# Four-layer conditional residual kernel in float32: GpSimd's splits of x in quarters, and its sums of layer-0 weights in halves

## What is computed

```python
# layer 0: one 256x256 weight matrix per row, mixed from 8
w = einsum('bg,got->bot', cond_8, weight * mask)
x = x + einsum('bnt,bot->bno', x, w) + bias
# layer 1: one of 8 experts per row (argmax), H = 512
x = x + (silu(x @ wu.T + bu) * (x @ wg.T + bg)) @ wd.T + bd
# layer 2: two of 8 experts per row (softmax weights) and a shared one, I = 1024
x = x + sum_u we[u] * ((gelu_tanh(x @ gate[u]) * (x @ up[u])) @ down[u])
# layer 3: base matrix plus LoRA mixed from 8 experts of rank 16
x = x + x @ (W_base + 2 * mixed_lora).T + b_base
```

## Time and profile before

| | us |
|---|---|
| median of 3 runs | 536.03 |
| lowest and highest | 536.0, 538.26 |
| span of the profiled execution, first to last instruction | 535.1 |
| median less that span | 0.9 |
| busy: PE, DVE, ACT, POOL | 506.0, 362.2, 241.3, 98.3 |

### The profile page before, as it was taken

The page is one execution under the profiler, slowest core; times in us unless marked ns, Lnnn a source line. Parts: engine busy times, 40 slices in busy tenths (PEclk is TensorE's granted clock), DMA queues, the critical chain, the costliest instruction groups (busy, mean ns, idle before and its releaser), DMA issues.

```text
span 535.1 us, 7145 instructions
## 1 busy us (share of the span) xinstructions
PE 506.0 (95%) x2155; PEld 405.9 (76%) x2155; DVE 362.2 (68%) x559; ACT 241.3 (45%) x372; POOL 98.3 (18%) x63
## 2 busy tenths in 40 slices
PE   6797988898999999899999998999999989999997
PEld 2475865686888888688888886888888778888886
DVE  4999999969865575755656557565665665656545
ACT  3464552462444445344444543444454444454430
POOL 1968694209400000200000002000000200000000
PEclk9999998998999999989999998999999999999999
DMA  8931312131423323232332332223223233230004
GB/s 253 385 96 32 106 49 72 53 106 59 119 88 103 103 88 91 69 105 88 99 107 80 98 108 67 88 88 118 88 88 110 66 105 101 88 92 25 0 1 158
DMA packets 20604, 51.38 MB, mean 96 GB/s; under 512 B 2928, under 2 KB 3568, under 8 KB 20592
## 3 DMA queue, kind: packets, MB, share of 16 engines
q1 hardware_dynamic: 20592, 51.24, 30.6%
HBM read 49.13 MB, written 2.10 MB: 96 GB/s over the span
## 4 chain that ended last, share of the span: by engine, by line
PE 85%; DVE 8%; issue 4%; DMA 2%; SPq 1%; ACT 1%; DVEq 0%
PE act_ps L290 10%; PE lin_ps L290 9%; PE lin_ps L291 9%; PE acc_ps L290 9%; PE lin_ps L292 9%; PE acc_ps L291 9%; PE act_ps L292 9%; PE act_ps L291 9%; PE acc_ps L292 9%; DMA w<-w_in 2%; DVE w_lo L619 1%; DVE hid_lo L637 1%; DVE w_sum L583 1%; DVE w_lo L611 1%; DVE hid L631 1%
## 5 line engine op out<-in xcount | busy, mean ns | idle before, releaser
L619 DVE TENSOR_TENSOR w_lo<-raw,w_hi 128x384 fp32r<-128x384 f32 (+1 forms) x222 | 152.5, 692 | 0.0
L629 DVE TENSOR_TENSOR hid<-lin_ps,act 128x512 f32<-128x512 f32 x96 | 66.2, 690 | 123.5 <-PE lin_ps L292 123.5
L429 ACT ACTIVATE hid_hi<-hid 128x512 fp32r<-128x512 f32 x112 | 70.8, 632 | 128.8 <-DVE hid L629 96.9
L423 ACT ACTIVATE act<-act_ps 128x512 f32<-128x512 f32 x96 | 57.4, 598 | 120.5 <-PE act_ps L292 120.5
L290 PE MATMUL act_ps<-x_hi,w_hi 128*128 (+1 forms) x228 | 90.0, 395 | 18.4 <-issue 13.5
L637 DVE TENSOR_TENSOR hid_lo<-hid,hid_hi 128x512 fp32r<-128x512 f32 x112 | 83.4, 745 | 21.8 <-ACT hid_hi L429 21.7
L417 ACT ACTIVATE w_hi<-raw 128x768 fp32r<-128x768 f32 x112 | 93.9, 838 | 0.0
L290 PE MATMUL lin_ps<-x_hi,w_hi 128*128 (+1 forms) x228 | 90.7, 398 | 0.0
L291 PE MATMUL lin_ps<-x_lo,w_hi 128*128 (+1 forms) x228 | 90.5, 397 | 0.0
L292 PE MATMUL lin_ps<-x_hi,w_lo 128*128 (+1 forms) x228 | 90.4, 397 | 0.0
L292 PE MATMUL act_ps<-x_hi,w_lo 128*128 (+1 forms) x228 | 89.5, 393 | 0.0
(11 more groups left out here) (91 smaller groups left out, 399.0 us busy)
## 6 DMA issues: line engine op xcount, KB each, us to landing
raw<-w_in SPq DMA_DIRECT2D x112, 384.0 KB, 3.0
w<-w_in SPq DMA_DIRECT2D x8, 256.0 KB, 7.6
x<-x_in SPq DMA_DIRECT2D x4, 512.0 KB, 8.2
out<-x SPq DMA_DIRECT2D x7, 256.0 KB, 2.4
mask<-mask_in SPq DMA_DIRECT2D x1, 256.0 KB, 6.6
base<-base_in SPq DMA_DIRECT2D x1, 256.0 KB, 10.1
out<-x SPq DMA_DIRECT2D x2, 128.0 KB, 2.2
lora_b<-lora_b_in SPq DMA_DIRECT2D x1, 128.0 KB, 6.9
```

The costliest lines, as they stand in the source:

```text
L423: act_e.activation(act[:, j % 2, :], act_ps[:, j % 2, :], func, bias=bias).then_inc(act_ready, 1)
L429: act_e.activation(hid_hi[:, j % 2, :], hid[:, j % 2, :], ACT.Copy).then_inc(hid_hi_ready, 1)
L619: ins = dve.tensor_tensor(w_lo[:, j % SPLIT, a:z], raw[:, j, a:z], w_hi[:, j % SPLIT, a:z].bitcast(F32), ALU.subtract)
L629: ins = dve.tensor_tensor(hid[:, j % 2, :], lin_ps[:, j % 2, :], act[:, j % 2, :], ALU.mult)
```

## The change

`split_lo` and `split_both` run over four quarters of 256 columns (`quarter`) in place of one instruction of 1024. The semaphores rise by 1 after every second quarter, and split_lo waits block by block. In `sum_w0` the addition of 512 columns becomes two of 256, and the semaphore rises after the second. The multiplication L793, the masking L782 and the weights of layer 3 stay as they are. No instruction changes its engine or its place in the order.

```diff
+            QT = T // 2
+            def quarter(t, b, q):
+                return t[:, b * CB * T + q * QT:b * CB * T + (q + 1) * QT]
             def split_lo(b, layer):
                 hi, lo, row = (x_hi, x_lo, b) if layer else (x0_hi, x0_lo, b % 2)
-                pool.wait_ge(x_hi_ready[layer], (b + 1) * CB)
-                pool.tensor_tensor(x_row(lo, row), x_row(x_flat, b), x_row(hi, row).bitcast(F32),
-                                   ALU.subtract).then_inc(x_lo_ready[layer], CB)
+                for q in range(CB * 2):
+                    if q % 2 == 0:
+                        pool.wait_ge(x_hi_ready[layer], b * CB + q // 2 + 1)
+                    ins = pool.tensor_tensor(quarter(lo, row, q), quarter(x_flat, b, q),
+                                             quarter(hi, row, q).bitcast(F32), ALU.subtract)
+                    if q % 2 == 1:
+                        ins.then_inc(x_lo_ready[layer], 1)
             def split_both(b, layer):
-                pool.tensor_copy(x_row(x_hi, b), x_row(x_flat, b)).then_inc(x_hi_ready[layer], CB)
+                for q in range(CB * 2):
+                    ins = pool.tensor_copy(quarter(x_hi, b, q), quarter(x_flat, b, q))
+                    if q % 2 == 1:
+                        ins.then_inc(x_hi_ready[layer], 1)
                 split_lo(b, layer)
...
-                        pool.tensor_tensor(w0_sum[:, b, :], w0_sum[:, b, :], w0_term[:, :],
-                                           ALU.add).then_inc(w0_pool, 1)
+                        for c in range(CB):
+                            cut = slice(c * D, (c + 1) * D)
+                            ins = pool.tensor_tensor(w0_sum[:, b, cut], w0_sum[:, b, cut], w0_term[:, cut], ALU.add)
+                        ins.then_inc(w0_pool, 1)
```

## The result

The changed kernel takes 513.79 us (median of 4 runs, 512.99 to 515.93) against 536.58 (4 runs, 536.0 to 538.26). The ratio is 0.9576, with a 95% interval of 0.9548 to 0.9603: 4.2% faster. The forecast was 515.5, within 509.5 to 522.0.

A forecast was written before the change was run, and what follows sets the result against it. TensorE (PE) bounds the kernel, busy 506.0 of 535.1 us, losing time to VectorE held by long GpSimd instructions and to low clock. Gains 14.1 + 6.4 = 20.5 give a 514.6 span, 515.5 median; range 509.5 to 522.

The forecast's parts named there:

- Turns at the boundary: VectorE instructions with two SBUF inputs wait for GpSimd's current instruction, then get in at every instruction boundary, needing 0.41 us.
- the mask rows: Trace at 77 us: between GpSimd instructions without pause, VectorE's w_lo ended at 77.45 and the mask took 1.03, not 0.74.
- the rival of the train: GpSimd's quarters run without letting VectorE in; row-end waits grow by 1.1 us in five episodes: 541.5 us, chance 0.05.
- Layer 2: Row-end episodes at 122, 224, 326 (4.0 us each) and 427 us (2.1) go: gain 14.1 us.
- The spare time: Row end at 224 us: w_lo complete at 223.1, TensorE wants it at 223.66, 0.6 us to spare.
- The two parts of the price: Each layer-2 row loses 4.0 us: 2.08 of TensorE waiting and 1.9 of low clock after it.
- The one at 103 us: TensorE's wait at 103 us, the same episode as at 224, goes with 0.3 to 0.5 to spare: gain 2.3 us.
- Layer 1: With layer 0, from 26.03 to 113.35 us: 13.9 us lost, 8.4 possible to win, 6.4 booked after a debit.
- The waits at 52 and 77: TensorE's layer-1 waits for w_lo go: 1.0 us at 52, 1.9 at 77, plus 1.9 for low clock behind 77.
- the debit of 2.0: Layer 1: 2.0 us taken off for row 3's mask, 2.5 late, and VectorE meeting GpSimd's layer-2 quarters past 90 us.
- The 0.9 between median and span: The median was taken to stand 0.9 us above the profiled span, turning 514.6 into the forecast 515.5.
- The halves of the sums: Halved layer-0 additions shorten VectorE's w_lo waits in layer 1; their gain was counted within the 8.4 us possible there.

The follow-up runs named there:

- casts_quartered: The kernel before with only the casts of x in quarters, each x_lo subtraction and the sums whole: 523.39 us, ratio 0.9738.
- subs_quartered: The kernel before with only the x_lo subtractions in quarters, each cast and the sums whole: 517.60 us, ratio 0.9639.
- sum_halves: The kernel before with only the additions of the layer-0 sums in halves, x in instructions of 1024: 534.82 us, ratio 0.9962.
- halves: The kernel before with x in two instructions of 512 columns, the sums whole: 519.88 us, ratio 0.9691.
- x_quarters: The changed kernel without the halved additions, so only x in quarters: 513.03 us, ratio 0.9548 to the kernel before.
- the finest cut: The kernel before with x in eight instructions of 128 columns, the sums whole: 516.14 us, ratio 0.9625.
- one wait more: x_quarters with GpSimd's layer-2 splits of rows 0 and 1 held until row 2 of layer 1 is added: 511.00 us, 0.9523 of the kernel before.

## Why the prediction was right

**Turns at the boundary: right.** The whole forecast hung on the mask rows, and casts_quartered and subs_quartered confirm it, each with a number of its own (1.42 and 2.41 us for the two w_lo). The Trainium skill's sentence (GPSIMD Engine Reference, section Instruction dispatch), that consecutive Pool instructions are no barrier between its cores, gave the rival of the train; no run here shows a train. Whether the cores wait for each other at a boundary can't be seen in these traces; in the rows shown, a waiting VectorE instruction got in at each.

**Layer 2: right, 14.1 forecast and 14.4 measured.** The spare time was put at 0.6 us and came out at 0.5; the upper bound of the cast was not needed. The two parts of the price, wait and clock, went together: with no wait the clock stayed full for the whole layer. Of the eight waits of 2.0 to 2.1 us in layer 2 of the kernel before and sum_halves, six had a stretch of low clock behind them; of the waits of 0.2 to 0.6 us at the row ends of layer 2 in casts_quartered, subs_quartered and halves, none had. So in layer 2 low clock came only behind a wait of 2 us, but not behind each. Why two of eight were spared isn't settled, nor why the longest wait in layer 1 of the kernel before, 2.31 us at 103 us, had full clock behind it too.

**The one at 103 us: right**, it is gone; the wait for hid_lo just ahead of it, 0.34 us at 101, is 0.44 at 94.

**Layer 1: the sign right, the size off, 6.4 forecast and 3.7 measured.** The waits at 52 and 77 and the low clock behind 77 went as said, and row 3's mask was late (ScalarE waited 2.2 us for it) but cost TensorE only 0.4, with 0.5 more for x_lo behind it. The step that failed is the debit of 2.0, which I placed at row 3 alone. The larger part stands at row 1: TensorE gets 1.67 us at 31, 0.4 at 35 (mask), 0.6 more at 42, and a stretch of low clock worth 1.7. There GpSimd's sums, x_lo of row 1 and mask of row 1 lie end to end from 24 us on, where the kernel before had GpSimd idle for 1.61 us ahead of that x_lo and 3.15 ahead of the mask, and TensorE comes there earlier, by what the start gained; how much each of the two adds wasn't tried apart. I had looked for crowding only where GpSimd was busy for 28.21 of 29.70 us, and not at the earlier stretch. As far as one trace of x_quarters shows, most of the shortfall belongs to the halves of the sums: without them layer 1 gains 5.8.

**The start: wrong.** "Before 26 us I book nothing, with 0.5 either way": measured 3.7. I had read the episodes of TensorE's waits and not the chain of VectorE before the first tile, in which the whole x_lo holds a multiplication (L590, 1.90 us against 0.86), w0_lo (L611, 1.85 against 0.76) then meets an addition that it now misses, and the whole additions hold VectorE's x_lo and what stands ahead of that. The two misses, 2.7 too much in layer 1 and 3.7 too little in the start, nearly cancel, and that is luck; 515.5 against 513.79 is closer than the terms deserve. The 0.9 between median and span compared two executions: where later runs of the kernel before list both, a span of 535.1 goes with a time of 536.9, so the profiled execution, with its loads late, was a slower one than the median of 536.03. The forecast took its 20.5 off that median all the same.

**The halves of the sums** were in the forecast as a gain in layer 1. They bring 1.5 us in the start and lose 2.2 in layer 1; in the medians nothing is left of either.

**GpSimd's own cost**: 11 us of added durations plus turns was the estimate, 24.2 the measurement (98.3 to 122.5), above the 10 to 20 that were named as a sign. If the 11 hold, the turns are the larger half. VectorE's w_lo in layer 1 came down to 803 ns, near the 750 named.

## What to carry to other kernels

When an engine off the path shares something with one on it, look at how long its single instructions are, not at its share of busy time: here GpSimd, busy for 18% of the time, cost 4%. Cut them to the slack of the waiting instruction (here w_lo had about 1 us: a subtraction takes 0.72 in quarters and 1.27 in halves), and no finer, since GpSimd's own results come later with each boundary; the finest cut lost 3 us. Where the other engine has no slack at all, moving the work to a later place can add to cutting it: one wait more gave 511.0 us, which no width did.

## What the hardware showed beyond that

- VectorE's instruction with one SBUF input and a scalar waits as well: L590 took 1.82 to 1.90 us beside GpSimd's whole x_lo in four kernels, and 0.57 to 0.93 beside quarters in eight traces. The one that reads PSUM and one SBUF tensor doesn't wait here: hid (L629) is 0.68 to 0.69 us in the middle of the row end as in all its 96 places.
- GpSimd's multiplication by a scalar holds VectorE for only a part of its own time. In the kernel before, timeline of POOL and DVE:

```profile
20.07 1.56 POOL L793 TENSOR_SCALAR w_term<-w,cols 128x512 f32<-128x512 f32 x1 [0.17 <-POOL w_sum L796]
20.10 1.20 DVE L583 SCALAR_TENSOR_TENSOR w_sum<-w,cols,w_sum 128x512 f32<-128x512 f32 x1
```

  The sum of VectorE (0.74 to 0.75 us by itself, and done 0.55 us after the end of an addition that holds it, at 23.84 us) ends at 21.30, 0.33 before the multiplication's end at 21.63, so it was let in an estimated 0.5 to 0.7 us after the start; with subtractions, additions and casts VectorE is let in at the end. Why they differ wasn't tried.
